# Turned rows of phases 3 and 5 stored from ScalarE's queue, and the rank loop's loads put ahead of its stores on SyncE

## What is computed

```python
h = relu(layernorm(x)); x = x + gcn2(h, src, dst, W1, b1, W2, b2)       # two graph convolutions
h = relu(layernorm(x)); x = x + concat([h, mean_of_neighbours(h)]) @ W.T + b
h = relu(layernorm(x)); x = x + sage2(h, src, dst, ...)                 # two layers, 128 -> 256 -> 128
h = relu(layernorm(x)); x = x + edge_mlp(h, src, dst, edge_weight, ...) # gelu, segment sum, gelu, layernorm
```

## Time and profile before

| | |
|---|---|
| median of 3 runs | 5862.0 us (5845.9 to 5865.1) |
| profiled execution, its own time | 5851.2 us |
| span of the profile | 5849.4 us, granted PE clock 0.91 |
| busy | PE 74%, DVE 59%, POOL 56%, ACT 53% |
| rank loop | about 440 to 1070 us |
| phase 3, phase 5 | about 2480 to 3060 us, 4030 to 4650 us |

### The profile page before, as it was taken

One profiled execution on the slowest core, in us unless ns is written; L12 is line 12 of the kernel. 1 busy time (PEld: TensorE's weight loads), 2 busy tenths in 40 slices (PEclk: granted clock), 3 DMA queues, 4 the chain that ended last, 5 costly groups with the idle time before them and its releaser, 6 DMA issues. The chain is left out here.

```text
span 5849.4 us, 136722 instructions
## 1 busy us (share of the span) xinstructions
PE 4302.6 (74%) x23129; PEld 3083.8 (53%) x23130; DVE 3428.6 (59%) x11290; ACT 3079.0 (53%) x6571; POOL 3264.7 (56%) x3244
## 2 busy tenths in 40 slices
PE   4556666577766888666649999998888537777777
PEld 1123333265555666555537777776667425455554
DVE  6875555443335877688843333334777426666666
ACT  7954444155545666466633333334666416666667
POOL 0006555275775557676764333454667577777771
PEclk8879999699988999889869999999999769999998
DMA  2212333144444555477754444455888646666665
GB/s 76 75 50 77 81 83 80 42 122 123 131 125 130 154 158 165 138 242 235 240 153 129 132 134 134 142 149 157 252 254 262 188 117 188 188 194 189 187 190 146
DMA packets 1061001, 879.24 MB, mean 150 GB/s; under 512 B 134328, under 2 KB 866000, under 8 KB 1060924
## 3 DMA queue, kind: packets, MB, share of 16 engines
q1 hardware_dynamic: 960572, 697.60, 39.5%
q0 software_dynamic: 100352, 180.83, 12.0%
HBM read 491.13 MB, written 412.40 MB: 154 GB/s over the span
## 5 line engine op out<-in xcount | busy, mean ns | idle before, releaser
L965 PE MATMUL banks<-M,OH 128*128 x9408 | 1322.5, 300 | 291.8 <-POOLq L593 167.4
L564 POOL DMA_INDIRECT M<-table_a,six x1176 | 1244.1, 1058 | 520.6 <-issue 327.5
L965 PEld LDWEIGHTS banks<-M,OH 128*128 128x128 f32 x9408 | 1246.0, 211 | 460.9 <-issue 432.0
L564 POOL DMA_INDIRECT M<-table_b,six x784 | 787.4, 1004 | 728.3 <-PE banks L965 499.6
L653 ACT ACTIVATE AG<-banks x1176 | 633.6, 591 | 771.6 <-PE banks L965 765.3
L1311 DVE TENSOR_TENSOR OH<-lane,dstrel 128x1024 f32<-128x1024 f32 x588 | 719.9, 1225 | 479.0 <-PE banks L965 348.4
L559 POOL DMA_INDIRECT edges_by_block<-pack,pos_i x392 | 376.0, 959 | 690.5 <-DVE pos_i L1184 591.5
L956 PE MATMUL banks<-zero_h 128*128 128x512 f16 x1176 | 360.8, 389 | 411.9 <-issue 254.6
L653 ACT ACTIVATE T<-banks 128x512 f32<-128x512 f32 (+1 forms) x588 | 295.9, 520 | 534.9 <-DMA table_b<-T 229.3
L883 PE MATMUL banks<-ident,HO 128*128 128x128 f32 x2352 | 380.8, 286 | 210.8 <-ACT HO L670 173.7
L564 POOL DMA_INDIRECT M<-table_pairs,dix x392 | 446.9, 1140 | 119.5 <-issue 101.8
(11 more groups left out here) (270 smaller groups left out, 7795.8 us busy)
## 6 DMA issues: line engine op xcount, KB each, us to landing
XB<-state SPq DMA_DIRECT2D x392, 256.0 KB
state<-T SPq DMA_DIRECT2D x196, 256.0 KB
table_a<-T SPq DMA_DIRECT2D x784, 64.0 KB
state<-Z SPq DMA_DIRECT2D x196, 256.0 KB
h_turned<-HT SPq DMA_DIRECT2D x196, 256.0 KB
table_pairs<-T SPq DMA_DIRECT2D x392, 128.0 KB
M<-messages SPq DMA_DIRECT2D x98, 512.0 KB, 4.2
XB<-in_x SPq DMA_DIRECT2D x390, 128.0 KB
```

The source lines that it names most:

```text
L564: nc.gpsimd.indirect_dma_start(out=M[:, slot, :], out_offset=None, in_=table, in_offset=bass.IndirectOffsetOnAxis(ap=idx, axis=0)).then_in ...
L965: last = mm(banks[:, ds(sums_at[k], P)], OH[:, b * US + k, :], source[:, ds(rows_at[k], P)], start=False, stop=False, skip_group_check=True)
```

## The change

Three lists are written in another order or shortened, and one step is new. In the rank loop SP now loads group n-1 first and stores group n-3 after it. In phases 3 and 5 the store of `HT` is gone from SP's list and is a step of ACT's list, behind `normed`. Both sides keep their semaphores: the step waits for `s_ht` and counts up `sh`.

```diff
-            staggered(sp, [(3, store0), (1, rows_for(s_ho))])
+            staggered(sp, [(1, rows_for(s_ho)), (3, store0)])
...
-            staggered(sp, [(4, whole_rows(3, h3_d, HT, (s_ht, "ht"), sh)), (3, whole_rows(3, states[3], Z, (s_var, "var"), sv)), (3, placed(3, tabs[1], HO, (s_ho, "ho"), st)),
+            staggered(sp, [(3, whole_rows(3, states[3], Z, (s_var, "var"), sv)), (3, placed(3, tabs[1], HO, (s_ho, "ho"), st)),
...
-            staggered(sp, [(3, whole_rows(5, states[5], Z, (s_var, "var"), sv)), (4, whole_rows(5, h5_d, HT, (s_ht, "ht"), sh)), (5, placed5),
+            staggered(sp, [(3, whole_rows(5, states[5], Z, (s_var, "var"), sv)), (5, placed5),
...
+            def turned_stored(d, table):
+
+                def do(i, b):
+                    g = 2 * i + b
+                    act.wait_ge(s_ht, g + (at(d, "ht") + 1))
+                    stand(act)
+                    act.dma_start(table[g], HT[:, b, :]).then_inc(sh[b], 16)
+                return do
...
-            staggered(act, [(4, turned(3)), (3, normed(3, Z)), (0, sums(2)), (2, deviations(3, (s_pre, at(3, "pre"))))])
+            staggered(act, [(4, turned(3)), (3, normed(3, Z)), (4, turned_stored(3, h3_d)), (0, sums(2)), (2, deviations(3, (s_pre, at(3, "pre"))))])
...
-            staggered(act, [(5, product(5)), (4, turned(5)), (3, normed(5, Z)), (0, sums(4)), (2, deviations(5, (s_pre, at(5, "pre"))))])
+            staggered(act, [(5, product(5)), (4, turned(5)), (3, normed(5, Z)), (4, turned_stored(5, h5_d)), (0, sums(4)), (2, deviations(5, (s_pre, at(5, "pre"))))])
```

## The result

| | us |
|---|---|
| before, median of 4 runs | 5856.97 (5845.89 to 5865.06) |
| after, median of 4 runs | 5676.53 (5675.90 to 5685.96) |
| ratio, 95% interval | 0.9697 (0.9676 to 0.9718) |
| after, profiled execution | 5677.07, span 5675.3, mean granted clock 0.92 |

The kernel became 3% faster, 180 us between the medians and 174 us between the two profiled executions (5851.2 and 5677.1).

The account below looks back on a forecast made before the run. Taken as bounds: the rank loop's loads behind stores, SP's full queue in phase 5, DVE's chain in phase 3. From 5851.2 us, -131 - 20 + 0 + 0 gave 5700.2; adding 6.5 made 5707 us, range 5665 to 5775.

Parts of the forecast that it names:

- Part 1: Rank loop: loads ahead of stores remove ACT's `XB` wait; POOL sets a 5.1 us turn instead of 6.45, gain 131 us.
- the ring: Rank loop: ACT's copy of `T1`, SP's store, then load, ACT's norm, PE's turning; 4.94 us from copy to landed data.
- the end of the loop: Last two groups after the rank loop: a few us of gain, counted only in the upper end of 140 us.
- Part 2: Phase 5: one issue less on SP's queue, turn 6.14 to 5.6-5.7 us, 40 turns of 0.5 us, gain 20 us.
- that sign: Phase 5: SP's turn falls to 5.5 to 5.7 us and SP now shows waits of its own.
- Parts 3 and 4: Phase 3's shorter SP queue gains 0 (end 10 us); 196 stores on ACT's queue cost 0 (end 20 us).
- 5.06 us for DVE's chain: Phase 3: DVE's busy time plus its 0.58 us own wait a turn, taken to set the 5.4 us turn.
- The base: Whole kernel: 6.5 us added because the three runs' mean, 5857.7, lay above the profiled execution's 5851.2 us.
- A: Rank loop: PE and DVE set the new turn at 5.6 us, gain 82 + 20, 5756 us; chance 0.12.
- B: Phase 5: the DMA engines set it, transfers take longer, the phase gains nothing, 5727 us; chance 0.14.
- C: Rank loop: loads still come as late as before, only phase 5's gain is left, 5838 us; chance 0.04.
- D: ACT's queue, phases 3 and 5: issues wait for the engine; slower from about 2.8 us each, 5903 at 3; chance 0.03.

Follow-up runs that it names:

- the kernel with the copies of `x`: Against the changed kernel, the four copies a turn of x into rank order moved from SP in phase 1 to ACT's queue in the rank loop: 5643.81 us.

## Why the prediction was right, point by point

**Part 1, the rank loop: right.** The wait for `XB` went whole (317 to under 1 us), POOL became the bound, and the turn is 5.07 us where I had 5.05 to 5.1. The term was 131 us, the packs gave 133.3. The order alone gave 146.7 us, so nothing else had a share in it. That the landing of a scatter isn't in the ring was right too: DVE's packs wait 104.6 us for it in 94 turns, and POOL hardly ever waits for DVE.

**The step that was mis-sized here: the end of the loop.** I counted pack to pack and put the last two groups at a few us, and only in the range. Timeline of DVE behind the last pack, which is at 1065.6 in the kernel before:

```profile
1066.02 0.60 DVE L1196 TENSOR_SCALAR ge<-iota_f,start 98x512 f32<-98x512 f32 x1
1080.61 0.49 DVE L1196 TENSOR_SCALAR ge<-iota_f,start 98x512 f32<-98x512 f32 x1 [13.99 <-PE banks L915]
```

and at 932.0 in the kernel after:

```profile
932.47 0.49 DVE L1205 TENSOR_SCALAR ge<-iota_f,start 98x512 f32<-98x512 f32 x1
938.47 0.50 DVE L1205 TENSOR_SCALAR ge<-iota_f,start 98x512 f32<-98x512 f32 x1 [5.51 <-PE banks L924]
```

`ge` begins the tables that the walk needs. PE makes the first product with it only behind its products of the last two groups, and before, these stood behind two more norms that waited 3.37 and 2.88 us for their `XB`. From the last pack to the second `ge` it was 15.0 us and is 6.5: 8.5 us of the 10.8. The steps of this kind that follow, which DVE and PE do in turn, take 12.9 us (938.47 to 951.40) where they took 16.3 (1080.61 to 1096.93); PE's granted clock was 0.55 in 1066 to 1090 us of before and is 0.78 in 932 to 956 of after. That makes 3.4 us, and 1 us is lost again in the rest of the way.

**Part 2, phase 5: right in its mechanism, 6 us short in its size.** The turn was put at 5.6 to 5.7 us and is 5.62 in the stretch of the table. The term was 40 turns of 0.5 us. What the phase gained didn't come as a number of equal turns: the starts of DVE's 98 `T` show another course. The first is at 4047.3 in before and 3900.0 in after, and the one 80 turns later, before and then after:

```profile
4529.69 0.69 DVE L1361 TENSOR_TENSOR T<-banks,be1bc 128x512 f32<-128x512 f32 x1
```

```profile
4347.47 0.69 DVE L1370 TENSOR_TENSOR T<-banks,be1bc 128x512 f32<-128x512 f32 x1
```

These are 482.4 and 447.5 us, so the kernel after is 34.9 us ahead by then, 0.44 us a turn. Five turns on it is 23.5, and 26.0 at the end. In between PE waits for POOL, as these waits of 4180 to 4430 us of the kernel after show; PE holds POOL back for 1.5 us there:

```profile
PE banks L974 <- POOLq L593: 23.9, 6, 7.5
...
POOL M L564 <- PE banks L974: 1.5, 5, 0.3
```

So what counts is POOL's own progress. Over the whole phase it was held back by PE for 63.8 us in before (4015 to 4625 us) and for 35.9 us in after (3868 to 4452 us):

```profile
POOL M L564 <- PE banks L965: 63.8, 23, 7.7
```

```profile
POOL M L564 <- PE banks L974: 35.9, 17, 7.4
```

That is 27.9 us less, near the phase's 26.0. The prediction named this limit and then took a flat 40 turns for it, which came out low. SP was to have waits of its own; it has none before 4350 us and 12 us in 3955 to 4405 us, so that sign failed: its queue was still full, and waited only in the kernel that has the second store out of it too.

**Parts 3 and 4: right.** Phase 3 changed by 0.3 us, and DVE's own wait stayed at 43.0 us. (The prediction's 5.06 us for DVE's chain stood against a turn of 5.4; the missing 0.3 us was not traced.) ACT's 196 issues cost next to nothing where they are; they took 0.34 us each, the value of SP's row. A second store in the same phase (state stores on ACT) also left ACT ahead. For four issues in a row the norm is too short to hide them, as the kernel with the copies of `x` shows.

**The base: wrong.** I added 6.5 us because the mean of the three runs lay that much over before's profiled execution. After's profiled execution lies at its own median, so between forecast and median this alone is 7 of the 30 us. The other 23 are the loop's end (11), phase 5 (6), the rank loop (2 to 3), phase 1 (2) and a us each in phase 4 and at the end.

**The rivals.** A fell (5.07 us a turn, with PE's granted clock at 1.00 in 500 to 550 us where before had 0.90). B fell by the lone store of phase 5 and by 285 GB/s, though each transfer did take longer with more of them in flight, as B had it (3.25 to 3.9 us). C fell by the timeline: the norm starts ahead of the load issued in its turn. D fell at 0.34 us an issue, against the 2.8 us from which it would have decided.

## What to carry to other kernels

On a queue that both loads and stores, look at what each load stands behind: a store waits for the newest result, a load needs only a free buffer. Where a turn's load comes after its store, a round trip of copy, store, load and landing sits in every turn, and swapping the two cost nothing here. A queue that shows no wait of its own over a whole stage is the first suspect for that stage's limit, as SP's was in phases 1 and 5; take issues out of it until it waits, and place them where the other engine's queue runs under a long instruction, no more of them than it covers. Then ask who takes over: in phase 5 a faster turn was worth only what POOL was still held back. And count the drain of a loop with its turns: the last groups run through the same ring.

## What was not expected of the hardware

- The length of phase 5 isn't steady where its code is the same: 603.0, 603.8 and 614.8 us in three kernels with the stores of before, 577.0, 579.8 and 585.0 in three with those of after (the last is 4454.6 - 3869.6 of the kernel with phase 1's copies moved). Differences of up to some 12 us in such a stage can't be read from one profile.
- PE's granted clock rose where the waits went: 1.00 in 500 to 550 us of the kernel after, with 37.92 us busy, against 0.90 with 33.53 us in the same stretch of before.
- The store of a group takes 0.34 us of SP's queue and 0.34 us of ACT's. Under a norm of 1.65 us it costs ACT's engine next to nothing (194 of 196 issues lie there), but four issues in a row made ACT's next copy wait 2.5 us.
- Twice the same program took over 7,000 us, once on a chip that had taken 5,864 us for it at another time, with ACT's and DVE's instructions as long as ever and several us between them in which only POOL worked. A gain that comes from an earlier load didn't show there at all (1.0011), one that takes issues out of a queue did (0.9926).
